# The last stage of a fused scan, attention and mixture-of-experts kernel: low parts moved to VectorE, gathered rows added tile by tile, last batch stored in four pieces

## The chip, the cores and the metric

One core of a Trainium2 chip. The metric is the device time of one execution in microseconds, as the median of three runs. The engines are TensorE (PE, with its weight loads as PEld), VectorE (DVE), ScalarE (ACT), GpSimd (POOL) and SyncE (SP), which issues most transfers.

## The reference, cut to what matters

Four batches of 512 rows, 512 wide. A selective scan over a context and an attention block come first; the change touches only what ends the program, the feed-forward part:

```
probs = softmax(h @ w_router); top_w, top_i = top_k(probs, 2)
y = (silu(h @ w_gate_e) * (h @ w_up_e)) @ w_down_e            # 8 experts, 352 wide
routed = sum over the 2 chosen experts of top_w * y
sh = (silu(h @ w_sh_gate) * (h @ w_sh_up)) @ w_sh_down        # shared expert, 1408 wide
x = x + routed + sigmoid(h @ w_sh_eg) * sh
out = x_before + tanh(g_ffn) * (that x)
```

## The kernel before, in words

**Numbers in two parts.** Each float32 operand of these products is split into a high part (rounded by ScalarE) and a low part (the value less the high part). A product is three passes: high by high, low by high, high by low. `split_product` (L627, matmuls at L631) issues them.

**The order of the feed-forward part.** The shared expert is 1408 wide, that is 11 pieces of 128. Nine of them come first (`NSB` = 3 passes), for all 16 row tiles (`NX` = 16, four per batch). Then follow 23 expert tiles of 256 routed rows (`NT` = 23), whose results go to the DRAM tensor `yg`. Then the last two pieces of the shared expert (`SHORT` = 2) are done batch by batch: eight steps s = 0 to 7, for batch b = s // 2. In each step `last_gate_up(s)` is two products of 12 matmuls on TensorE, `last_tanh(s)` runs on ScalarE, `last_act(s)` is two instructions on VectorE (L2174, L2179), `last_round(s)` writes the high part `lah` on ScalarE (L1655), and `last_rest(s)` writes the low part `lal` on GpSimd (L2464). `last_down(b)` is four tiles of six matmuls each. TensorE's order is: steps 0 to 3, down(0), steps 4 and 5, down(1), steps 6 and 7, down(2), down(3); one expert tile's down product lies behind step 0.

**The adding.** `shared_add(NSB, b)` (L2144) adds the four tiles of down(b) from two PSUM banks into the rows `xs`; a tile of `last_down` waits until the tile two before it has been added, since it writes the same bank (`pe.wait_ge(d_acc, m - 1)`, L1152). `combine(b)` (L2190) adds the two gathered expert rows of each row, eight instructions for a batch: all four tiles for the first choice, then all four for the second. It waits for all eight gathers of the batch (`y_in`).

**The gathers.** `gather(b, first, end_)` (L2471) issues indirect DMAs on GpSimd, two for each row tile, eight for a batch, 32 in all, into `yab`, which holds two batches. Batch 2 waits until batch 0 is combined, batch 3 until batch 1 is. GpSimd's order is: low parts 0 and 1, a wait for the last expert tile's store, gathers 1 to 4, low part 2, gathers 5 to 10, low part 3, gathers 11 to 16, low parts 4 and 5, gathers 17 to 24, low part 6, gathers 25 to 28, low part 7, gathers 29 to 32.

**VectorE's order.** Step 3 is followed by the adds of batch 0, step 4 by combine(0), step 5 by the adds and the combine of batch 1; steps 6 and 7 follow, then adds and combine of batch 2, then of batch 3.

**The stores.** SP stores each batch as one transfer of 1 MB (L619), when it is added and combined.

The names of the waits: `f_ah`, `f_al` count high and low parts, `f_a` the activations, `d_mm` and `d_acc` the down tiles made and added, `comb` the combine instructions.

Of the kernel before, what the change touches and what calls it, by code (L numbers as in the profile page):

```python
# [6 lines left out]
B, L, H = 4, 512, 512  # L7
# [7 lines left out]
T4 = L // P  # L15
KC = H // P
NCH = -(-EI // P)
SHORT = -(-SI // P) - (NU - NE - 1) * NCH
EW = NCH * P
NSH = NU - NE  # L20
NSB = NSH - 1
TT = 2 * P
NT = 2 * B * L // TT + NE - 1
NX = B * T4
# [19 lines left out]
def build(nc, x_in, ctx_in, gates_in, w_in_in, chan_in, xproj_in, dtproj_in, watt_in, bqk_in,  # L44
          bv_in, wln_in, route_in, wffn_in, rope_in, perm_in, ident_in, mask_in, iota_in, out,
          b_scratch, x2d, h2d, hhd, xg, yg):
    f32, f32r, bf16, u32, i32 = (mybir.dt.float32, mybir.dt.float32r, mybir.dt.bfloat16,
                                 mybir.dt.uint32, mybir.dt.int32)
    ALU, ACT, AX = mybir.AluOpType, mybir.ActivationFunctionType, mybir.AxisListType
# [3 lines left out]
    with ctx:  # L53
        def sem(name):
            return ctx.enter_context(nc.semaphore(name))
# [25 lines left out]
        sg = keep("sg", [P, NX])  # L81
# [12 lines left out]
        slot = keep("slot", [P, 2, NX], u32)  # L94
# [47 lines left out]
        rtw = mid("rtw", [P, KC, ROUTE])  # L142
        rth = mid("rth", [P, KC, ROUTE], f32r)
        rtl = mid("rtl", [P, KC, ROUTE], f32r)
# [92 lines left out]
        def xs_rows(first, last):  # L237

            if last <= EARLY * T4:
                return xs_early[:, first:last, :]  # L240
            return xs_late[:, first - EARLY * T4:last - EARLY * T4, :]

        def xs_row(t):
            return xs_rows(t, t + 1)[:, 0, :]
# [30 lines left out]
        hT_ready, y_acc, y_z, x1_done = sem("states_transposed"), sem("y_added"), sem("y_gated"), sem("x1_done")  # L275
        wraw_in = [sem("att_weights_loaded0"), sem("att_weights_loaded1")]
        wah_done, wal_done = sem("att_weights_hi"), sem("att_weights_lo")
        rt_split = sem("router_split")
        a_bn, a_mv, a_norm, a_hp = [sem("att_" + n) for n in ("stats", "meanvar", "norm", "scaled")]
        h1_mm, h1_hi, h1_lo = sem("h1_transposed"), sem("h1_hi"), sem("h1_lo")  # L280
        v_mm, v_done = sem("v_product"), sem("v_ready")
# [44 lines left out]
        def parts(u):  # L326
            return NCH if u < NSB else SHORT
# [24 lines left out]

        def last_step(u):
            return sum(parts(v) for v in range(u + 1)) * B

        def gate_up_split(e, job, c):
            if c < 2:
# [72 lines left out]
        def _(sp):  # L430
# [121 lines left out]
            def moe_stage():  # L552
# [57 lines left out]
                for b in range(1, B):  # L610
# [2 lines left out]
                        sp.dma_start(part[:].bitcast(f32), hhd[j, b]).then_inc(hh_ld[b], 16)  # L613
                    if b == 1:
                        tile_out(NT - 1)
                for b in range(B):
                    sp.wait_ge(comb, 2 * T4 * (b + 1))
                    sp.wait_ge(d_acc, NX * NSB + T4 * (b + 1))
                    sp.dma_start(out[b], xs_rows(T4 * b, T4 * b + T4)).then_inc(stored, 16)  # L619

            moe_stage()
            sp.wait_ge(stored, B * 16)

        @block.tensor
        def _(pe):
# [399 lines left out]
            shared = shared_pieces()  # L1026
            first_scan()
            pe.wait_ge(attc_in, 80)
            pe.wait_ge(rt_split, 2)
            pe.wait_ge(wal_done, KC)  # L1030
            for r in range(B):
                round_(r, r + 1)
# [156 lines left out]
        def _(act):  # L1189
# [507 lines left out]
            make_consts()  # L1697
            first_scan()
            act.wait_ge(attc_in, 80)
            nc.scalar.activation(rth[:], rtw[:], ACT.Copy).then_inc(rt_split, 1)  # L1700
            for r in range(B):
                round_(r, r + 1)
            for step in range(4):
# [5 lines left out]
        def _(dve):  # L1709
# [336 lines left out]
            def moe_stage():  # L2046
# [89 lines left out]
                def shared_add(u, b):  # L2136
                    for tt in range(T4):
                        m, t = NX * u + T4 * b + tt, T4 * b + tt
                        dve.wait_ge(d_mm, m + 1)
                        if m == T4 * EARLY:  # L2140
                            dve.wait_ge(xs_ld, 32 * B)
                        if u:
                            dve.wait_ge(d_acc, m - NX + 1)
                        nc.vector.scalar_tensor_tensor(xs_row(t), FD[m % 2][:], sg[:, t:t + 1], xs_row(t),  # L2144
                                                       ALU.mult, ALU.add).then_inc(d_acc, 1)
# [19 lines left out]
                def tile_out(i):  # L2165
                    dve.wait_ge(y_mm, 2 * i + 2)
                    if i >= 2:
                        dve.wait_ge(y_st[i % 2], 16 * (i // 2))
                    nc.vector.tensor_copy(ysb[:, i % 2, 1, :], FD[1][:]).then_inc(y_sv, 1)
# [8 lines left out]
                    dve.wait_ge(f_al, n - 1)  # L2178
                    nc.vector.tensor_tensor(fa[:, n % 2, :], FU[n % 2][:], ft[:, n % 2, :], ALU.mult).then_inc(f_a, 1)  # L2179

                def combine(b):
                    dve.wait_ge(y_in[b % 2], 16 * 2 * T4 * (b // 2 + 1))
                    for j in range(2):
                        for tt in range(T4):
                            t = T4 * b + tt
                            if j:
                                dve.wait_ge(comb, 2 * T4 * b + tt + 1)
                            else:
                                dve.wait_ge(d_acc, NX * NSB + t + 1)
                            nc.vector.scalar_tensor_tensor(xs_row(t), yab[:, b % 2, tt, j, :], w01[:, j, t:t + 1],  # L2190
                                                           xs_row(t), ALU.mult, ALU.add).then_inc(comb, 1)

# [18 lines left out]
                for i in range(NT):  # L2211
# [6 lines left out]
                    if i:  # L2218
                        tile_out(i - 1)
                    low_down(NSB + i + 1)  # L2220
                for s in range(SHORT * B):
                    last_act(s)
                    if s == 0:
                        tile_out(NT - 1)
                    if s == 3:
                        shared_add(NSB, 0)
                    if s == 4:
                        combine(0)
                    if s == 5:
                        shared_add(NSB, 1)  # L2230
                        combine(1)
                for b in range(2, B):
                    shared_add(NSB, b)
                    combine(b)

            dve.wait_ge(const_in, 96)
            dve.wait_ge(consts, 7)
# [2 lines left out]
                                        ALU.mult, ALU.mult).then_inc(consts, 1)  # L2240
            first_scan()
            dve.wait_ge(attc_in, 80)
            dve.wait_ge(rt_split, 1)
            nc.vector.tensor_tensor(rtl[:], rtw[:], rth[:].bitcast(f32), ALU.subtract).then_inc(rt_split, 1)
            dve.wait_ge(zfill, 16 * 12)
            dve.wait_ge(wal_done, KC)
            for r in range(B):
# [9 lines left out]
        def _(pool):  # L2257
# [179 lines left out]
            def moe_stage():  # L2437
# [22 lines left out]
                def last_rest(s):  # L2460
                    b, c = divmod(s, SHORT)
                    n = ENDING + s
                    pool.wait_ge(f_ah, n + 1)
                    nc.gpsimd.tensor_tensor(lal[:, b % 2, c, :], fa[:, n % 2, :], lah[:, b % 2, c, :].bitcast(f32),  # L2464
                                            ALU.subtract).then_inc(f_al, 1)

                def gather(b, first, end_):

                    for r in range(first, end_):
                        tt, j = divmod(r, 2)  # L2470
                        nc.gpsimd.indirect_dma_start(yab[:, b % 2, tt, j, :], None, yg, bass.IndirectOffsetOnAxis(  # L2471
                            ap=slot[:, j, T4 * b + tt:T4 * b + tt + 1], axis=0)).then_inc(y_in[b % 2], 16)

                for s, (u, b, c) in enumerate(steps):
                    if s < SE:
# [21 lines left out]
                last_rest(1)  # L2497
                for i in range(2):
                    pool.wait_ge(y_st[i], 16 * ((NT + 1 - i) // 2))
                gather(0, 0, 4)  # L2500
                last_rest(2)
                gather(0, 4, 8)
                gather(1, 0, 2)
                last_rest(3)
                gather(1, 2, 8)
                last_rest(4)
                last_rest(5)
                pool.wait_ge(comb, 2 * T4)
                gather(2, 0, 8)
                last_rest(6)  # L2510
                pool.wait_ge(comb, 4 * T4)
                gather(3, 0, 4)
                last_rest(7)
                gather(3, 4, 8)

            for row, value in ((mhalf, -0.5), (eps5, 1e-5), (eps6, 1e-6), (mone, -1.0), (perh, 1.0 / H),
                               (one, 1.0), (onee, 1.0 + 1e-6), (epsp, 1e-5 * 1e-6)):
# [86 lines left out]
```

## Time and profile before

| what | value |
|---|---|
| median of three runs | 1787.9 us (1785.01 to 1793.58) |
| the profiled execution | 1790.59 us |
| its span | 1788.8 us, so 1.8 us lie around it |
| mean granted TensorE clock | 0.902 |
| PE busy | 1503.7 us, 84% |
| DVE busy | 1166.9 us, 65% |
| ACT busy | 916.2 us, 51% |
| POOL busy | 810.2 us, 45% |

Busy shares are averages over stages that differ in what limits them. All that the change moves lies in the last 100 us of the span, so the rows below are of that stretch. In the timeline a row is: start, length, engine, line, operation, written tile, read tiles, shape and count; in brackets the idle time before it and what ended that.

### The profile page before, as it was taken

What the parts mean: (1) busy time and instruction counts of PE and PEld (TensorE: products, weight loads), DVE (VectorE), ACT (ScalarE), POOL (GpSimd) and SP (SyncE); (2) the same over time, 40 slices, a digit from 0 to 9 for tenths busy, and PEclk for the clock granted to TensorE, in tenths of its full rate; (3) what the DMA queues carried; (4) which work ended last, traced back from release to release, by engine and by line L of the source; (5) the groups of instructions that cost most, each with busy time, mean ns of one, the idle gap of its engine ahead of it and who ended that gap; (6) DMA issues with size and microseconds to landing.
All of it is one profiled execution on the core that took longest, in us unless ns stands there. A gap on an engine that the chain in (4) does not pass through costs nothing.

```text
span 1788.8 us, 26797 instructions
## 1 busy us (share of the span) xinstructions
PE 1503.7 (84%) x9168; PEld 1150.6 (64%) x9168; DVE 1166.9 (65%) x1699; ACT 916.2 (51%) x2038; POOL 810.2 (45%) x807
## 2 busy tenths in 40 slices
PE   5677967788777789677878998799999999999994
PEld 2344645565445556455655666688787999999973
DVE  5987589996699985899945444432324666566545
ACT  5675457764467753567724663221213666666510
POOL 1992266542466532565413211243422555555444
PEclk8789968899878899788988999899999999999997
DMA  4460001111011111011132004721311877777464
GB/s 168 153 229 19 25 23 55 54 43 54 7 35 55 54 36 31 19 47 54 37 123 95 30 32 160 293 77 59 110 37 65 307 243 253 261 241 253 155 221 165
DMA packets 94664, 195.76 MB, mean 109 GB/s; under 512 B 8945, under 2 KB 25841, under 8 KB 91201
## 3 DMA queue, kind: packets, MB, share of 16 engines
q1 hardware_dynamic: 89408, 177.26, 29.1%
q0 software_dynamic: 5120, 16.78, 2.8%
q8 instruction: 75, 1.23, 0.3%
q14 instruction: 61, 0.49, 0.1%
HBM read 140.40 MB, written 53.61 MB: 108 GB/s over the span
## 4 chain that ended last, share of the span: by engine, by line
PE 55%; DVE 16%; issue 15%; POOL 7%; ACT 5%; DMA 1%; SPq 1%; DVEq 0%; ACTq 0%; POOLq 0%
PE scores L631 21%; PE bank L631 14%; DVE HS L1770 6%; DVE YA L1781 4%; PE bank L705 3%; PE bank L775 3%; POOL GB L2281 2%; PE bank L790 2%; ACT bank L1269 2%; PE bank L825 2%; PE scores L762 2%; POOL yab L2471 2%; PE scores L749 1%; PE bank L1092 1%; PE scores L765 1%
## 5 line engine op out<-in xcount | busy, mean ns | idle before, releaser
L2281 POOL TENSOR_TENSOR GB<-DU,BB 128x512 f32<-128x512 f32 x256 | 326.8, 1298 | 36.1 <-DVE DL L1752 21.2
L1770 DVE TENSOR_TENSOR_SCAN HS<-bank,GB 128x512 f32<-128x512 f32 x224 | 272.0, 1214 | 20.3 <-ACT bank L1269 17.6
L705 PE MATMUL bank<-ident,HS 128*128 128x128 f32 x860 | 165.8, 325 | 120.9 <-DVE YA L1781 104.9
L705 PEld LDWEIGHTS bank<-ident,HS 128*128 128x128 f32 x860 | 115.2, 165 | 166.3 <-DVE YA L1781 129.8
L1269 ACT ACTIVATE bank<-DL,aneg 128x512 f32<-128x512 f32 x224 | 154.7, 691 | 110.0 <-DVE HS L1770 108.2
L775 PE MATMUL bank<-ident,EX 128*128 128x128 f32 x640 | 131.5, 306 | 34.2 <-ACT PT L1314 20.9
L631 PE MATMUL scores<-xth,wgh 128*128 128x256 f32 x552 | 158.1, 286 | 2.2 <-DVE fa L2162 1.3
L1781 DVE SCALAR_TENSOR_TENSOR YA<-bank,Ct,YA 128x512 f32<-128x512 f32 x199 | 147.0, 738 | 14.2 <-PE bank L705 12.8
L631 PE MATMUL scores<-xth,wgl 128*128 128x256 f32 x552 | 156.1, 283 | 0.0
L631 PE MATMUL scores<-xtl,wgh 128*128 128x256 f32 x552 | 156.1, 283 | 0.0
L1314 ACT ACTIVATE PT<-bank 128x128 f32<-128x128 f32 (+3 forms) x256 | 110.3, 431 | 72.0 <-PE bank L775 64.9
L1306 ACT ACTIVATE EX<-scores,nm 128x128 f32<-128x128 f32 (+3 forms) x256 | 132.3, 521 | 22.4 <-DVE nm L1826 21.7
L775 PEld LDWEIGHTS bank<-ident,EX 128*128 128x128 f32 x640 | 79.8, 154 | 75.0 <-issue 47.0
L2426 POOL TENSOR_TENSOR wgl<-wgr,wgh 128x768 fp32r<-128x768 f32 x54 | 110.9, 2057 | 30.4 <-ACT wgh L1580 30.4
L2443 POOL TENSOR_TENSOR fal<-fa,fah 128x512 fp32r<-128x512 f32 x30 | 38.8, 1293 | 162.7 <-ACT fah L1609 162.5
L2324 POOL TENSOR_TENSOR ctl<-cn,cth 128x128 fp32r<-128x128 f32 x64 | 29.3, 458 | 180.7 <-ACT cth L1325 180.7
L631 PEld LDWEIGHTS scores<-xth,wgh 128*128 128x128 f32 x552 | 105.7, 191 | 3.6 <-DVE fa L2162 1.7
L631 PE MATMUL scores<-hah,wgh 128*128 128x512 f32 x272 | 106.7, 392 | 1.0 <-issue 1.0
L631 PE MATMUL scores<-hal,wgh 128*128 128x512 f32 x272 | 106.5, 391 | 0.0
L631 PE MATMUL scores<-hah,wgl 128*128 128x512 f32 x272 | 106.3, 391 | 0.0
L631 PEld LDWEIGHTS scores<-xtl,wgh 128*128 128x128 f32 x552 | 105.7, 192 | 0.9
L631 PEld LDWEIGHTS scores<-xth,wgl 128*128 128x128 f32 x552 | 105.7, 191 | 0.0
(294 smaller groups left out, 3798.6 us busy)
## 6 DMA issues: line engine op xcount, KB each, us to landing
wgr<-wffn_in SPq DMA_DIRECT2D x108, 384.0 KB, 6.5
wdr<-wffn_in SPq DMA_DIRECT2D x81, 256.0 KB, 3.1
BB<-b_scratch SPq DMA_DIRECT2D x64, 256.0 KB, 3.3
xr<-xg SPq DMA_DIRECT2D x23, 512.0 KB, 5.8
yg<-ysb SPq DMA_DIRECT2D x23, 512.0 KB, 6.5
xg<-V SPq DMA_DIRECT2D x11, 1024.0 KB, 5.8
hah<-hhd SPq DMA_DIRECT2D x5, 1024.0 KB, 14.1
hal<-hhd SPq DMA_DIRECT2D x5, 1024.0 KB, 16.1
```

What stands on the lines that cost most here:

```text
L631: mm = nc.tensor.matmul(out_, parts[a](k), rhs_parts[b](k), start=(k == 0 and j == 0), stop=(k == n - 1 and j == 2))
L705: mm = nc.tensor.transpose(state_bank(s, q)[:, et * P:(et + 1) * P], HS[:, n % 2, et, tt * P:(tt + 1) * P], ident[:])
L762: nc.tensor.matmul(SB[:, a, 0:W], QK[r:r + HD, m, i * P:(i + 1) * P], QK[r:r + HD, 4 + m, 0:W], start=True, stop=False)
L775: mm = nc.tensor.transpose(turned_bank(b, v)[:, kb * P:(kb + 1) * P], EX[:, a, kb * P:(kb + 1) * P], ident[:])
L1269: nc.scalar.activation(decay_bank(s, k), DL[:, et, :], ACT.Exp, scale=aneg[:, et, n:n + 1]).then_inc(dA_ready, 1)
L1306: nc.scalar.activation(EX[:, a, 0:W], SB[:, a, 0:W], ACT.Exp, bias=nm[:, a:a + 1], accum_out=rs[:, q % 2, a:a + 1]).then_inc(ex_done, 1)
L1314: nc.scalar.activation(PT[:, a, 0:W], turned_bank(b, v)[:, 0:W], ACT.Copy).then_inc(pt_done, 1)
L1770: nc.vector.tensor_tensor_scan(HS[:, n % 2, et, :], decay_bank(s, k), GB[:, k % 4, :], 0.0, ALU.mult, ALU.add).then_inc(scan_done, 1)
L1781: nc.vector.scalar_tensor_tensor(YA[:, tt, :], state_bank(s, q), Ct[:, tt, n:n + 1], YA[:, tt, :], ALU.mult, ALU.add).then_inc(y_acc, 1)
L2281: nc.gpsimd.tensor_tensor(GB[:, k % 4, :], DU[:, et, :], BB[:, n % 2, :], ALU.mult).then_inc(gb_ready, 1)
L2426: nc.gpsimd.tensor_tensor(wgl[raw][:, c, :], wgr[raw][:, c * 2 * EW:(c + 1) * 2 * EW], wgh[raw][:, c, :].bitcast(f32), ALU.subtract).then_ ...
L2443: nc.gpsimd.tensor_tensor(fal[:, b % 2, c, :], fa[:, s % 2, :], fah[:, b % 2, c, :].bitcast(f32), ALU.subtract).then_inc(f_al, 1)
```

## The change

It does five things, all in the last stage.

1. Low parts 2 to 7 (`last_rest`) run on VectorE; parts 0 and 1 stay on GpSimd, ahead of the gathers.
2. GpSimd issues its 32 gathers without other work between them. A gather for batch 2 or 3 waits only for the same tile of the batch two before.
3. `combine` works tile by tile (both choices of one row tile after another), and its tiles are put between steps, low parts and adds in an order written out by hand. For batch 2 the combine comes before the add of the down product, for the others behind it.
4. The very last gather has a semaphore of its own, `y_last`, waited for only ahead of the very last combine instruction. To have one free, the two increments of `rt_split`, early in the program, go to `consts`.
5. Batch 3 is stored as four transfers of one row tile (256 KB), each as soon as its tile is done.

```diff
+        def added_first(t):
+            return t < 2 * T4 or t >= NX - T4
...
-                for b in range(B):
+                for b in range(B - 1):
                     sp.wait_ge(comb, 2 * T4 * (b + 1))
                     sp.wait_ge(d_acc, NX * NSB + T4 * (b + 1))
                     sp.dma_start(out[b], xs_rows(T4 * b, T4 * b + T4)).then_inc(stored, 16)
+                for t in range(NX - T4, NX):
+                    sp.wait_ge(comb, 2 * t + 2)
+                    sp.wait_ge(d_acc, NX * NSB + t + 1)
+                    sp.dma_start(out[B - 1, :, t % T4:t % T4 + 1, :], xs_rows(t, t + 1)).then_inc(stored, 16)
...
-            pe.wait_ge(rt_split, 2)
+            pe.wait_ge(consts, 7 + T4 + 2)
...
-                def combine(b):
-                    dve.wait_ge(y_in[b % 2], 16 * 2 * T4 * (b // 2 + 1))
-                    for j in range(2):
-                        for tt in range(T4):
-                            t = T4 * b + tt
+                def last_rest(s):
+                    b, c = divmod(s, SHORT)
+                    n = ENDING + s
+                    dve.wait_ge(f_ah, n + 1)
+                    dve.wait_ge(f_al, n)
+                    nc.vector.tensor_tensor(lal[:, b % 2, c, :], fa[:, n % 2, :], lah[:, b % 2, c, :].bitcast(f32),
+                                            ALU.subtract).then_inc(f_al, 1)
+
+                def add_last(b, first, end_):
+                    for t in range(T4 * b + first, T4 * b + end_):
+                        m = NX * NSB + t
+                        dve.wait_ge(d_mm, m + 1)
+                        if added_first(t):
+                            dve.wait_ge(d_acc, m - NX + 1)
+                        else:
+                            dve.wait_ge(comb, 2 * t + 2)
+                        nc.vector.scalar_tensor_tensor(xs_row(t), FD[m % 2][:], sg[:, t:t + 1], xs_row(t),
+                                                       ALU.mult, ALU.add).then_inc(d_acc, 1)
+
+                def combine(b, first, end_):
+                    dve.wait_ge(y_in[b % 2], 16 * (2 * T4 * (b // 2 + 1) - (b == B - 1)))
+                    for tt in range(first, end_):
+                        t = T4 * b + tt
+                        dve.wait_ge(d_acc, NX * (NSB if added_first(t) else NSB - 1) + t + 1)
+                        for j in range(2):
                             if j:
-                                dve.wait_ge(comb, 2 * T4 * b + tt + 1)
-                            else:
-                                dve.wait_ge(d_acc, NX * NSB + t + 1)
+                                dve.wait_ge(comb, 2 * t + 1)
+                            if j and t == NX - 1:
+                                dve.wait_ge(y_last, 16)
...
-                for s in range(SHORT * B):
+                last_act(0)
+                tile_out(NT - 1)
+                for s in range(1, 4):
                     last_act(s)
-                    if s == 0:
-                        tile_out(NT - 1)
-                    if s == 3:
-                        shared_add(NSB, 0)
-                    if s == 4:
-                        combine(0)
-                    if s == 5:
-                        shared_add(NSB, 1)
-                        combine(1)
-                for b in range(2, B):
-                    shared_add(NSB, b)
-                    combine(b)
+                last_rest(2)
+                add_last(0, 0, 4)
+                last_rest(3)
+                combine(0, 0, 2)
+                last_act(4)
+                combine(0, 2, 3)
+                last_rest(4)
+                combine(0, 3, 4)
+                last_act(5)
+                add_last(1, 0, 1)
+                last_rest(5)
+                add_last(1, 1, 4)
+                combine(1, 0, 3)
+                last_act(6)
+                combine(1, 3, 4)
+                last_rest(6)
+                combine(2, 0, 2)
+                last_act(7)
+                add_last(2, 0, 1)
+                last_rest(7)
+                combine(2, 2, 3)
+                add_last(2, 1, 3)
+                combine(2, 3, 4)
+                add_last(2, 3, 4)
+                add_last(3, 0, 4)
+                combine(3, 0, 4)
...
                 last_rest(1)
                 for i in range(2):
                     pool.wait_ge(y_st[i], 16 * ((NT + 1 - i) // 2))
-                gather(0, 0, 4)
-                last_rest(2)
-                gather(0, 4, 8)
...
-                last_rest(7)
-                gather(3, 4, 8)
+                for b in range(B):
+                    for tt in range(T4):
+                        if b >= 2:
+                            pool.wait_ge(comb, 2 * (T4 * (b - 2) + tt) + 2)
+                        gather(b, 2 * tt, 2 * tt + 2)
```

## Rows read from the trace of the kernel before

**Rows 1.** The chain that ended last, 1756 to 1789 us, shares by line.
```profile
by line: issue 35.0%; POOL yab L2471 25.3%; DVE xs_late L2190 14.3%; DMA yab<-yg,slot 10.4%; POOL lal L2464 7.7%; DVEq L53 2.0%; POOLq L53 0.7%
```

**Rows 2.** Timeline of GpSimd: low parts and gathers.
```profile
1705.63 1.29 POOL L2464 TENSOR_TENSOR lal<-fa,lah 128x512 fp32r<-128x512 f32 x1 [8.23 <-ACT lah L1655]
1707.07 0.99 POOL L2471 DMA_INDIRECT yab<-yg,slot  x1 [0.15 <-issue]
...
1710.90 0.96 POOL L2471 DMA_INDIRECT yab<-yg,slot  x1 [0.30 <-issue]
...
1715.86 0.94 POOL L2471 DMA_INDIRECT yab<-yg,slot  x1 [0.30 <-issue]
1723.63 0.94 POOL L2471 DMA_INDIRECT yab<-yg,slot  x1 [6.83 <-issue]
...
1731.42 1.02 POOL L2471 DMA_INDIRECT yab<-yg,slot  x1 [0.30 <-issue]
...
1740.30 0.95 POOL L2471 DMA_INDIRECT yab<-yg,slot  x1 [5.28 <-issue]
...
1757.89 0.95 POOL L2471 DMA_INDIRECT yab<-yg,slot  x1 [4.85 <-issue]
...
1775.66 0.95 POOL L2471 DMA_INDIRECT yab<-yg,slot  x1 [5.01 <-issue]
```

**Rows 3.** Timeline of VectorE: adds, combines and the last steps.
```profile
1715.69 1.51 DVE L2144 SCALAR_TENSOR_TENSOR xs_early<-bank,sg,xs_early 128x512 f32<-128x512 f32 x2
...
1727.52 6.08 DVE L2190 SCALAR_TENSOR_TENSOR xs_early<-yab,w,xs_early 128x512 f32<-128x512 f32 x8 [0.50 <-DMA yab<-yg,slot]
...
1749.04 0.69 DVE L2174 SCALAR_TENSOR_TENSOR ft<-ft,scores 128x512 f32<-128x512 f32 x1
1749.76 0.69 DVE L2179 TENSOR_TENSOR fa<-scores,ft 128x512 f32<-128x512 f32 x1
...
1761.22 6.74 DVE L2190 SCALAR_TENSOR_TENSOR xs_late<-yab,w,xs_late 128x512 f32<-128x512 f32 x8 [3.47 <-DMA yab<-yg,slot]
...
1779.11 5.39 DVE L2190 SCALAR_TENSOR_TENSOR xs_late<-yab,w,xs_late 128x512 f32<-128x512 f32 x8 [3.98 <-DMA yab<-yg,slot]
```

**Rows 4.** Timeline of TensorE: matmuls around its waits in the last stage.
```profile
1735.64 0.50 PE L631 MATMUL bank<-wdh,lah 128*128 128x512 f32 x1 [2.54 <-DVE xs_early L2144]
...
1740.09 0.40 PE L631 MATMUL scores<-hah_odd,wgh 128*128 128x512 f32 x1
...
1750.98 0.39 PE L631 MATMUL bank<-wdh,lah 128*128 128x512 f32 x1
...
1766.99 0.77 PE L631 MATMUL bank<-wdh,lah 128*128 128x512 f32 x1 [10.02 <-POOL lal L2464]
...
1771.47 0.39 PE L631 MATMUL bank<-wdh,lah 128*128 128x512 f32 x1
...
1773.96 0.39 PE L631 MATMUL bank<-wdh,lal 128*128 128x512 f32 x1
```

**Rows 5.** Stretches: busy time of each engine, granted clock, DMA share, GB/s.
```profile
1740.00:1751.00 11.00, 11.00 (x51) 9.07 (x50) 7.43 (x11) 1.12 (x2) 9.01 (x9) 1.00 0.39 108
...
1767.00:1771.00 4.00, 4.00 (x10) 3.16 (x11) 1.71 (x3) 0.00 (x0) 3.03 (x3) 0.56 0.60 174
```

**Rows 6.** Groups by line in the last stage: the low part on GpSimd, and VectorE's nearest.
```profile
L2464 POOL TENSOR_TENSOR lal<-fa,lah 128x512 fp32r<-128x512 f32 x8 | 10.3, 1290 | 13.4 <-ACT lah L1655 13.4
...
L2043 DVE TENSOR_TENSOR wdl<-wdr,wdh 128x512 fp32r<-128x512 f32 x2 | 1.3, 689 | 0.0
```

**Rows 7.** Timeline of SP's transfers in the last stage.
```profile
1713.72 0.32 SPq L613 DMA_DIRECT2D hah_odd<-hhd  x1
...
1733.63 15.86 SPq L619 DMA_DIRECT2D out<-xs_early  x2
1767.99 16.88 SPq L619 DMA_DIRECT2D out<-xs_late  x2
```

**Rows 8.** Transfers of line 487, 256 KB each, whole span.
```profile
DMA to landing us min/median/max: 2.2/3.5/4.4
```

More of the change, by code:

```diff
@@ L277, in build @@
         wah_done, wal_done = sem("att_weights_hi"), sem("att_weights_lo")
-        rt_split = sem("router_split")
+        y_last = sem("last_row_gathered")
         a_bn, a_mv, a_norm, a_hp = [sem("att_" + n) for n in ("stats", "meanvar", "norm", "scaled")]
@@ L619, in moe_stage @@
                     sp.dma_start(out[b], xs_rows(T4 * b, T4 * b + T4)).then_inc(stored, 16)
+                for t in range(NX - T4, NX):
+                    sp.wait_ge(comb, 2 * t + 2)
+                    sp.wait_ge(d_acc, NX * NSB + t + 1)
+                    sp.dma_start(out[B - 1, :, t % T4:t % T4 + 1, :], xs_rows(t, t + 1)).then_inc(stored, 16)
             moe_stage()
-            sp.wait_ge(stored, B * 16)
+            sp.wait_ge(stored, (B - 1 + T4) * 16)
         @block.tensor
@@ L1699, in _ @@
             act.wait_ge(attc_in, 80)
-            nc.scalar.activation(rth[:], rtw[:], ACT.Copy).then_inc(rt_split, 1)
+            nc.scalar.activation(rth[:], rtw[:], ACT.Copy).then_inc(consts, 1)
             for r in range(B):
@@ L2242, in _ @@
             dve.wait_ge(attc_in, 80)
-            dve.wait_ge(rt_split, 1)
-            nc.vector.tensor_tensor(rtl[:], rtw[:], rth[:].bitcast(f32), ALU.subtract).then_inc(rt_split, 1)
+            dve.wait_ge(consts, 7 + T4 + 1)
+            nc.vector.tensor_tensor(rtl[:], rtw[:], rth[:].bitcast(f32), ALU.subtract).then_inc(consts, 1)
             dve.wait_ge(zfill, 16 * 12)
@@ L2471, in gather @@
                         nc.gpsimd.indirect_dma_start(yab[:, b % 2, tt, j, :], None, yg, bass.IndirectOffsetOnAxis(
-                            ap=slot[:, j, T4 * b + tt:T4 * b + tt + 1], axis=0)).then_inc(y_in[b % 2], 16)
+                            ap=slot[:, j, T4 * b + tt:T4 * b + tt + 1], axis=0)).then_inc(y_last if (b, r) == (B - 1, 2 * T4 - 1) else y_in[b % 2], 16)
                 for s, (u, b, c) in enumerate(steps):
@@ L2499, in moe_stage @@
                     pool.wait_ge(y_st[i], 16 * ((NT + 1 - i) // 2))
-                gather(0, 0, 4)
-                last_rest(2)
-                gather(0, 4, 8)
[L2503 to L2512, printed above, removed]
-                last_rest(7)
-                gather(3, 4, 8)
+                for b in range(B):
[3 more added lines that the diff above has]
+                        gather(b, 2 * tt, 2 * tt + 2)
             for row, value in ((mhalf, -0.5), (eps5, 1e-5), (eps6, 1e-6), (mone, -1.0), (perh, 1.0 / H),
```

## The prediction

> **What bounds the kernel now.** I read first the chain that ended last, because the change lies wholly in the last 100 us. Over the final 33 us [rows 1] TensorE is not in it at all: issuing on GpSimd and the gathers hold most, VectorE's combine 14.3%, GpSimd's low parts 7.7%. So the question is GpSimd's queue, and its timeline was next [rows 2]. Gathers follow one another at about 1.28 us (1707.07 to 1710.90 is three steps), except that gathers 8, 16, 24 and 32 each stand behind 4.85 to 6.83 us of idle time which no semaphore of the program explains. Those four rows are the clock of the ending. They lie 16.7, 17.6 and 17.8 us apart. In the first of these cycles GpSimd does one low part between gathers, in the other two it does two each, at 1.29 us [rows 6].
>
> What follows from the late gathers is read in VectorE's and TensorE's timelines. Combine(2) starts at 1761.22, 3.33 us behind gather 24, combine(3) at 1779.11, 3.45 us behind gather 32 [rows 2, 3]. TensorE stands 10.02 us ahead of down(3), for low part 7 [rows 4], which waits on GpSimd behind gather 28. TensorE ends at 1774.35 (1773.96 + 0.39), so the last 14.4 us are gather 32, eight combines (5.39 us) and a 1 MB store: 1784.50 to 1788.8, 4.3 us [rows 2 to 4]. SP issues the four stores in those places [rows 7].
>
> TensorE itself needs less. 48 matmuls from 1740.09 to 1750.98 are 0.227 us each; a down tile of six is 1.36, a step of 24 is 5.44.
>
> **The change part by part.**
>
> *The semaphore of the router split*: same producers, same order, one count shared. It adds no instruction; zero. What covers it is nothing, and nothing is needed.
>
> *Low parts 2 to 7 on VectorE*: nearest row is VectorE's own subtraction of this shape, 0.69 us [rows 6]. Six of them are 4.1 us more on VectorE, and 6 x 1.29 = 7.7 us off GpSimd. Where VectorE is idle they cost nothing. Part 2 is the first that shows: it stands between step 3 and the first add of batch 0, so the add at 1715.69 [rows 3] comes 0.7 later and TensorE's third tile of down(0) with it, 0.7 us. TensorE has slack for that, since what ends the program comes from the gathers.
>
> *The gathers*: gather 1 stays at 1707.07, for low part 1 ahead of it stays on GpSimd [rows 2]. Gather 7 moves from 1715.86 to 1707.07 + 6 x 1.27 = 1714.7. The stall ahead of gather 8 spans the loads of `hah_odd` (2 MB, issued from 1713.72 [rows 7]); with the stall unchanged gather 8 is at 1714.7 + 0.94 + 6.83 = 1722.5, with the shortest stall (4.85) at 1720.5, with no gain at 1723.6. I take 1722.5, as the loads stay where they were.
>
> A cycle of eight gathers is then 7 x 1.27 + 0.95 = 9.85 us plus the stall. The stall is not shown without a store beside it. From below: data land about 3.4 us after a gather's start, 2.5 after its end, so 2.5 is the least if the stall waits for the seventh to land: cycle 12.4. From above: 5.28 gives 15.1. The 1 MB stores still fall near gathers 16 and 24, so I stay nearer the upper rows: 14.2. Gather 16 then starts at 1736.7, gather 24 at 1750.9, gather 32 at 1765.1, against 1740.3, 1757.9 and 1775.7.
>
> *What VectorE does with it.* In tile order the second instruction of a pair waits for the first to end. The pair of a step shows that price: 0.72 from start to start (1749.04, 1749.76) for an instruction of 0.69; a combine lasts 0.75, so about 0.78 and then 0.66 (5.39 less 0.75, over seven), 1.44 a tile, 5.8 a batch instead of 5.4 [rows 3]. Combine(0) can start at 1722.5 + 3.9 = 1726.4 and holds step 4 until 1729.3; TensorE is then in step 5 until 1731. Its third tile of down(1) waits for the add that stands behind step 5, to about 1736.5, much as at 1735.64 before [rows 4]. Combine(1) starts at about 1740, step 6 at 1746.5, step 7's product ends at 1751.5. So nothing up to there is later than the gathers by more than a microsecond, and TensorE's idle time of 2.5 us returns.
>
> The new wait is combine(2, 0, 2): it stands ahead of step 7 in VectorE's queue. Behind it are step 7, the first add of batch 2 and low part 7, and on them wait the third tile of down(2), ScalarE's high part, and down(3). All start from gather 24: 1750.9 + 3.4 = 1754.3. From there, in order:
> - two tiles of combine 2.9, step 7 1.4, add 0.75, restart 0.05: TensorE starts the third tile at 1759.4, after some 5 us of idle time;
> - 12 matmuls after such a gap took 1766.99 to 1771.47, 4.5 us instead of 2.7, the granted clock 0.56 in that stretch [rows 4, 5], between the levels of 1.2 and 2.4 GHz; between the two tiles lies the wait for an add behind low part 7 and a combine, 0.6; then four tiles, 5.45: 1769.9;
> - visible end and last add, 0.2 + 0.7: 1770.8;
> - four tiles of combine(3), 5.8: 1776.6. `y_last` comes at 1765.1 + 3.45 = 1768.6 and is not waited for;
> - the last store is 256 KB. Such a transfer took at least 2.2 us [rows 8], against 4.3 for 1 MB: 1778.8.
>
> The median of line 487 is 3.5 [rows 8], but beside other traffic; at the end only the three small stores ahead of it run, so I take 2.2 and keep 3.5 for the range.
>
> Sum: span 1778.8 against 1788.8, 10.0 us less (0.56%). Split: 2.1 from the store, 7.9 from where the combine of batch 3 starts (1770.8 against 1779.1, less 0.4 for tile order). The profiled execution was 1790.59 with 1.8 around the span; the median of the runs is 1787.9. So 1777.9, written as 1778.
>
> A rule that speaks against the change concerns the last term but one. The row first: gathers beside combines last 1.02 us (1731.42) against 0.94 alone, and two batches of combines took 6.08 and 6.74 us against 5.39, each with a GpSimd low part beside them [rows 2, 3]. So here GpSimd's subtraction delays VectorE by 0.7 to 1.4, and a gather loses 0.08 at most. The Trainium skill (SBUF — State Buffer, Who interferes with whom) says that a VectorE instruction with two SBUF inputs contends with a GpSimd instruction that reads SBUF, and that the second one blocks fully. By it the combines gain (the subtractions are gone from GpSimd), and gathers, if they read their row numbers through that way, would each lose a whole VectorE instruction; and the sum by it would be 1790.6 with one instruction each.
>
> **The rivals.**
> - *Gathers 16 and 24 gain only the low parts, and stores hit them as hard as the stores of before* (cycle 15.1 to 16.7, or the clock staying low into down(3)). For: every stall seen has a store or load beside it. Against: the store of batch 0 now leaves near 1734, when gather 15 has mostly landed. With 16.7 twice, gather 24 is at 1755.9 and the end at 1783.8; time 1783, no measurable change. Chance 0.32, with the milder form of the next rival but one in it.
> - *The stall is mostly the stores*, and away from them it is 2.5 to 3.5 us: cycle 12.4 to 13.3, gather 24 at 1747.3 to 1749.1, TensorE's gap shrinks to 2 or 3 us, end 1774.9 to 1777; time 1775. Chance 0.14.
> - *Slower: gathers blocked by VectorE.* VectorE now runs six more instructions with two SBUF inputs, and often two behind one another without a gap (1.44 us for a tile of combine). If each of the 16 gathers between 8 and 24 is held for such a pair, that is 16 x 1.44 = 23 us: combine(2) starts at 1777.3 and the end is 1801.8, time 1801. With one instruction of 0.74 each it is 11.8 us, end 1790.6, time 1790, no change to measure. It eats the gain from 10.0 / 16 = 0.63 us per gather and decides for slower from (10.0 + 8.9) / 16 = 1.2. For it stand the stretched combines, against it the 0.08 seen on gathers. Chance of the slower form 0.07.
> - *The change frees nothing*, since the stalls are not work of GpSimd: then only the 7.7 us of subtractions go, which is what the forecast counts; the store alone is worth 2.1 (1786). Contained in the first rival.
>
> **How the numbers follow.** The forecast has 0.47: 1778, own range 1775 to 1782. A measurement of this kernel can tell about 0.5%, 8.9 us, so faster means below 1779.0. The second rival is faster; of the forecast's own spread some four fifths lies below that line. Faster 0.53, same 0.40, slower 0.07. For the range 1773 takes in the shorter cycle, 1786 the first rival with the store of 3.5 us; outside are the slower rival and some tails.
>
> **What the profile after would show.** GpSimd: 32 gathers, still with a stall at 8, 16, 24 and 32, the cycles 13.3 to 15.1, gather 24 before 1753. VectorE: combine(2)'s first instruction waiting for the gathers and starting near 1754. TensorE: one gap of 4 to 6 us ahead of the third tile of down(2), none ahead of down(3), end near 1770. Four stores of 256 KB, the last landing 2.2 us behind the last combine. It is wrong if the stalls grow when gathers are issued closer together, if gathers last over 1.1 us, if the last combine waits for `y_last`, or if TensorE's clock stays at the lower level for the six last tiles.

## The result and the profile after

The changed kernel took 1782.4 us (median of eight), the kernel before 1790.97 beside it; the ratio is 0.996, with an interval of 0.9944 to 0.9976. So it is faster by 0.4%, clear of noise but under the 0.5% that the prediction took as the bound: by that bound the time is the same, which had a chance of 0.40, and not faster, which had 0.53. Forecast were 10.0 us less. The profiled execution has a span of 1783.5 us, 5.3 less than before.

Executions differ by several microseconds ahead of the last stage: in the traces of this study step 0 starts anywhere between 1683.7 and 1694.1 us, in kernels that differ up to there in no more than one semaphore, the places of small tiles and the descriptor space. So I compare **the ending**: from the first matmul of step 0 to the end of the span. (That matmul starts 0.19 us ahead of VectorE's copy of the expert tile before, which is easy to find in each trace.) Before it is 1687.7 to 1788.8, 101.1 us; after it is 1688.8 to 1783.5, 94.7 us. The change is worth 6.4 us of the forecast 10.0.

GpSimd's timeline after, which answers to [rows 2]:

```profile
1708.17 0.99 POOL L2517 DMA_INDIRECT yab<-yg,slot  x1 [0.15 <-issue]
...
1715.75 0.95 POOL L2517 DMA_INDIRECT yab<-yg,slot  x1 [0.30 <-issue]
1724.57 0.94 POOL L2517 DMA_INDIRECT yab<-yg,slot  x1 [7.88 <-issue]
...
1728.32 1.32 POOL L2517 DMA_INDIRECT yab<-yg,slot  x1 [0.30 <-issue]
...
1738.66 0.94 POOL L2517 DMA_INDIRECT yab<-yg,slot  x1 [3.42 <-issue]
...
1752.09 1.43 POOL L2517 DMA_INDIRECT yab<-yg,slot  x1 [3.18 <-issue]
...
1765.60 0.95 POOL L2517 DMA_INDIRECT yab<-yg,slot  x1 [3.25 <-issue]
```

The stalls are still ahead of gathers 8, 16, 24 and 32, but three of them are 3.2 to 3.4 us instead of 5. The cycles are 14.1, 13.4 and 13.5 us. In the ending's own time gather 24 stands at 63.3 (forecast 63.2, before 70.2).

The chain of waits after, from gather 24 to the combine of batch 3 (start, length, what):

```profile
1748.92 3.18 issue
1752.09 5.96 DMA yab<-yg,slot
...
1758.08 0.76 DVE xs_late L2220
...
1758.86 1.42 DVE xs_late L2220 x2
...
1760.38 0.60 issue
1760.98 0.69 DVE ft L2182
...
1761.84 0.47 issue
1762.31 0.75 DVE xs_late L2206
...
1763.10 11.19 PE bank L639 x36
...
1774.35 0.63 issue
1774.99 0.75 DVE xs_late L2220
```

This is the path of the prediction, link by link: gather 24, two tiles of combine, step 7, one add, then 36 matmuls (six tiles) and the last batch. One link is far longer than forecast: the gather took 5.96 us to land, not 3.4. SP's timeline says what was beside it:

```profile
1735.90 16.56 SPq L623 DMA_DIRECT2D out<-xs_early  x2
1769.68 0.33 SPq L623 DMA_DIRECT2D out<-xs_late  x1
1776.54 4.68 SPq L627 DMA_DIRECT2D out<-xs_late  x4
```

The first row is two stores. The second of them ends its issue at 1735.90 + 16.56 = 1752.46, and an issue lasts 0.33: batch 1's 1 MB leaves at 1752.13, within 0.1 us of gather 24's start. TensorE after, answering to [rows 4], and two stretches answering to [rows 5]:

```profile
1737.91 0.80 PE L639 MATMUL bank<-wdh,lah 128*128 128x512 f32 x1 [3.09 <-DVE xs_early L2206]
...
1763.10 0.79 PE L639 MATMUL bank<-wdh,lah 128*128 128x512 f32 x1 [7.01 <-DVE xs_late L2206]
...
1773.89 0.39 PE L639 MATMUL bank<-wdh,lal 128*128 128x512 f32 x1
```

```profile
1757.00:1767.00 10.00, 3.90 (x9) 2.69 (x10) 8.57 (x13) 0.63 (x1) 5.08 (x6) 0.57 0.56 180
1767.00:1771.00 4.00, 4.00 (x16) 3.21 (x15) 2.73 (x4) 0.00 (x0) 0.00 (x0) 0.80 0.40 135
```

The wait ahead of down(3) has gone and one of 7.01 us stands ahead of down(2)'s third tile, on VectorE's add. The granted clock is 0.57 in the stretch that holds it, and 0.50, the lower level, from 1763.1 to 1768.0. The last combine and the landing of the small stores:

```profile
1774.99 5.88 DVE L2220 SCALAR_TENSOR_TENSOR xs_late<-yab,w,xs_late 128x512 f32<-128x512 f32 x8
```

```profile
DMA to landing us min/median/max: 2.2/2.2/2.3
```

VectorE ends at 1780.87, the span 2.6 us later.

### The profile page after: what moved, and what is told of

Its sections match the earlier page's. It is cut to its first block, busy times and chain, and to the rows that moved or that the text cites. A ratio compares the mean times of both kernels' runs of the same rounds, so it can differ in the third digit from the quotient of the medians.

```text
span 1783.5 us, 26815 instructions
## 1 busy us (share of the span) xinstructions
PE 1498.1 (84%) x9168; PEld 1147.3 (64%) x9168; DVE 1171.1 (66%) x1705; ACT 915.1 (51%) x2038; POOL 803.1 (45%) x801
## 3 DMA queue, kind: packets, MB, share of 16 engines
q8 instruction: 75, 1.23, 0.3%
## 4 chain that ended last, share of the span: by engine, by line
PE 55%; DVE 17%; issue 14%; ACT 6%; POOL 5%; DMA 2%; SPq 1%; DVEq 0%; ACTq 0%; POOLq 0%
PE scores L639 21%; PE bank L639 15%; DVE HS L1778 6%; DVE YA L1789 4%; PE bank L713 3%; PE bank L783 3%; PE bank L798 2%; PE scores L770 2%; ACT bank L1277 2%; PE bank L833 2%; POOL GB L2327 2%; POOL yab L2517 1%; PE scores L757 1%; PE bank L1100 1%; DVE nm L1834 1%
## 6 DMA issues: line engine op xcount, KB each, us to landing
hah<-hhd SPq DMA_DIRECT2D x5, 1024.0 KB, 14.2
```

## The experiments

The table gives the ratio to the kernel before, its interval, and the ending of the profiled execution. The experiments follow in the order of what they tell.

| kernel | ratio | interval | ending, us | gather 24 | TensorE ends |
|---|---|---|---|---|---|
| before | 1 | | 101.1 | 70.2 | 86.7 |
| after | 0.996 | 0.9944 to 0.9976 | 94.7 | 63.3 | 85.5 |
| late_store | 0.9943 | 0.993 to 0.9956 | 92.0 | 63.5 | 82.7 |
| step7_first | 0.9924 | 0.9908 to 0.994 | 88.0 | 63.3 | 78.5 |
| step7_late_store | 0.9941 | 0.9912 to 0.997 | 88.1 | 63.4 | 78.6 |
| low_parts_only | 0.9972 | 0.9956 to 0.9988 | 96.2 | 62.3 | 85.9 |
| tile_stores_only | 1.0003 | 0.9989 to 1.0018 | 100.2 | 70.1 | 86.6 |
| ring_before_b | 0.9923 | 0.9902 to 0.9944 | 91.1 | 58.5 | 80.7 |
| ring_after | 0.9889 | 0.9871 to 0.9907 | 83.5 | 49.5 | 74.2 |
| ring_order | 0.99 | 0.9882 to 0.9918 | 84.5 | 52.4 | 75.0 |
| ring_comb3 | 0.9888 | 0.9862 to 0.9913 | 81.3 | 49.7 | 75.7 |

(The last two columns are in the ending's own time.)

Each ending is that of one execution. `before` and `tile_stores_only` are alike up to the last store, and their gather 32 stands at 88.0 and 88.5, so differences of half a microsecond between endings mean nothing. The ratios are of all runs; the two measures differ by up to 3.8 us (ring_before_b: 13.8 us by its ratio, 10.0 in the ending), which is as wide as the intervals. Three more versions, ring16, ring16b and ring_before, had only four of the eight small tiles elsewhere; they did not fit in SBUF and have no time.

**late_store: is it the store that holds gather 24 back?**

```diff
                 for b in range(B - 1):
+                    if b == 1:
+                        sp.wait_ge(y_in[0], 16 * 4 * T4)
```

> The kernel after, but SP issues batch 1's store only when gather 24 has landed. Measured by the length of the ending, from the first matmul of step 0 to the end of the span: 101.1 us before (1687.7 to 1788.8), 94.7 after (1788.8 to 1783.5 with a start at 1688.8). Theory 'the store hits gather 24': in the profile after, gather 24 and the 1 MB store of batch 1 start together at 1752.1 and the combine waits 5.96 us for the gather instead of the 3.4 of an undisturbed one; without the store beside it combine(2) starts 2.6 us earlier and the ending is 92.1. Rival 'VectorE holds the gather back' (gather 24 lasted 1.43 us beside a low part and combine): the landing stays near 6 us and the ending at 94.7.

The ending is 92.0, against 92.1 forecast. The gather and the combine behind it:

```profile
1751.07 0.94 POOL L2519 DMA_INDIRECT yab<-yg,slot  x1 [3.34 <-issue]
```

```profile
1751.07 3.29 DMA yab<-yg,slot
```

The start of gather 24 has not moved (63.5 against 63.3); its landing takes 3.29 us instead of 5.96. The gather itself also lasts 0.94 here and not 1.43, for its neighbours on VectorE have moved too; the landing of 5.96 counts from the gather's start, so the 0.5 of the longer issue can be part of it. The pair step7_first and step7_late_store below has no such difference: there gather 24 lasts 0.95 and 0.94, and it lands after 4.8 us with batch 1's store issued 0.65 us ahead of it, after 3.3 without:

```profile
DMA to landing us min/median/max: 4.8/4.8/4.8
```

```profile
DMA to landing us min/median/max: 3.3/3.3/3.3
```

So the store is the cause, of 1.5 us in that pair and of 2.2 to 2.7 here.

**step7_first: is it VectorE's order that makes the gather matter?**

```diff
         def added_first(t):
-            return t < 2 * T4 or t >= NX - T4
+            return True
...
-                combine(2, 0, 2)
                 last_act(7)
                 add_last(2, 0, 1)
                 last_rest(7)
-                combine(2, 2, 3)
-                add_last(2, 1, 3)
-                combine(2, 3, 4)
-                add_last(2, 3, 4)
-                add_last(3, 0, 4)
+                add_last(2, 1, 4)
+                combine(2, 0, 2)
+                add_last(3, 0, 1)
+                combine(2, 2, 3)
+                add_last(3, 1, 2)
+                combine(2, 3, 4)
+                add_last(3, 2, 4)
                 combine(3, 0, 4)
```

> The kernel after, but on VectorE step 7, its low part and the adds of batch 2 stand ahead of combine(2), and all adds come before the combines. Theory 'VectorE's order makes TensorE wait for gather 24': TensorE's 7.0 us of idle time ahead of the third tile of down(2) shrinks to under 1 us and its lower clock goes, down(3) ends near 1765 instead of 1774.3; combine(2) (5.8), four adds (2.8) and combine(3) (5.8) follow from the gather's landing at 1758, then a store of 2.6: ending 86.3, 8.4 less. Rival 'the gathers alone set the end': ending 94.7 as after.

88.0, 6.7 less than after, of the 8.4 expected. TensorE's long wait has gone:

```profile
1768.85 0.50 PE L639 MATMUL bank<-wdh,lah 128*128 128x512 f32 x1 [1.68 <-DVE xs_late L2206]
```

That is the only wait over 1 us left behind down(1), now in down(3), for an add that stands behind two tiles of combine. TensorE ends at 78.5 instead of 85.5. This wait is not what the forecast missed. Combine(2) starts at 71.0 in the ending's time, where the forecast had gather 24's landing (1758 in after, 69.2), because it stands behind the fourth add of batch 2, which waits for TensorE:

```profile
1764.49 0.75 DVE L2206 SCALAR_TENSOR_TENSOR xs_late<-bank,sg,xs_late 128x512 f32<-128x512 f32 x1 [0.62 <-PE bank L639]
1765.16 2.98 DVE L2220 SCALAR_TENSOR_TENSOR xs_late<-yab,w,xs_late 128x512 f32<-128x512 f32 x4
```

From there to its end VectorE shows no idle time, so these 1.8 us account for the 1.7 that are missing.

**step7_late_store: are these two causes or one?** Both edits together.

> Both edits on the kernel after: step 7, its low part and batch 2's adds ahead of combine(2), and batch 1's store only when gather 24 has landed. With the order alone the ending was 88.0, with combine(2) starting at 71.0 and TensorE waiting 1.7 us ahead of down(3)'s third tile. Theory 'two causes, partly the same wait': combine(2) starts at 66.8, that wait goes, TensorE ends at 76.8, ending 86.3. Rival 'independent': 88.0 less the 2.8 of the store, 85.2. Rival 'the store no longer matters': 88.0.

88.1 against 88.0: with step 7 ahead, the store's collision costs nothing. The rival that the store no longer matters holds, and my own forecast of 86.3 was wrong: combine(2) started at 71.0 and 71.1, since it now waits for the fourth add of batch 2 and not for the gather. The 1.8 us that I expected did not come; TensorE's wait in down(3) is still there (1.67), beside a VectorE that is busy throughout.

**low_parts_only: what do the low parts bring without the new order?**

```diff
                 for s in range(SHORT * B):
                     last_act(s)
+                    if s >= 2:
+                        last_rest(s)
...
-                gather(0, 0, 4)
-                last_rest(2)
...
+                for b in range(B):
+                    if b >= 2:
+                        pool.wait_ge(comb, 2 * T4 * (b - 1))
+                    gather(b, 0, 8)
```

> The kernel before with one part of the change: low parts 2 to 7 on VectorE, each right behind its step, and GpSimd with only gathers between, a batch at a time; VectorE's order, the combine and the stores are those of before. Theory 'the gain is the gathers', the new order takes part of it back': gather 24 at about 51 to 53 us of the ending's start plus 12, as after; steps 6 and 7 stand ahead of combine(2) as before, so TensorE does not wait for it; combine(3) starts when gather 32 lands: ending 90, 11 less than before's 101.1 and 4.7 less than after's. Rival 'the order by tiles brings the gain': ending over 96.

96.2: the theory's 90 fell by 6.2, and the number is the rival's (over 96), though not for the rival's reason, as the parts add up below. Gather 24 is as early as after (62.3), but does not set the end:

```profile
1736.40 0.50 PE L631 MATMUL bank<-wdh,lah 128*128 128x512 f32 x1 [4.04 <-DVE xs_early L2144]
...
1765.93 0.79 PE L631 MATMUL bank<-wdh,lah 128*128 128x512 f32 x1 [4.09 <-DVE xs_late L2144]
```

TensorE waits twice for an add behind a whole combine, 4.0 and 4.1 us, with a granted clock of 0.66 and 0.50 in the 3.6 and 4.0 us behind them. I had left both out of the 90. So this part alone gives 4.9 of the 6.4 us.

**tile_stores_only: what does the store in four pieces bring?** The kernel before, with batch 3 stored in four pieces.

```diff
+                for t in range(NX - T4, NX):
+                    sp.wait_ge(comb, 2 * NX - T4 + t % T4 + 1)
+                    sp.wait_ge(d_acc, NX * NSB + t + 1)
+                    sp.dma_start(out[B - 1, :, t % T4:t % T4 + 1, :], xs_rows(t, t + 1)).then_inc(stored, 16)
```

> The kernel before with one part of the change: batch 3 stored by four transfers of 256 KB, the combine unchanged (all first choices, then all second, so the four tiles end 0.66 us apart). From the last combine's end to the end of the span it was 4.3 us before and 2.64 after. Theory: 2.6 to 2.8, ending 99.4 to 99.6 instead of 101.1. Rival (four transfers issued within 2 us stand behind each other): no gain, 101.

From the last combine's end to the end of the span it is 2.85 us, against 4.3 before: 1.45 less. In this execution gather 32 came 0.6 later, so the ending shows 0.9. The ratio, 1.0003, can't tell so little from nothing. Adding the parts: 96.2 less 1.5 is 94.7, the ending after. So by this subtraction the new order of VectorE, with the descriptor space as it was, added nothing; no run has the order alone.

**ring_after: what are the stalls?** Nothing of the program's order is changed; eight small tiles are placed elsewhere to free 1 KB a partition.

```diff
-    nc = bacc.Bacc("TRN2", target_bir_lowering=False, num_devices=1, dynamic_dma_scratch_size=1024)
+    nc = bacc.Bacc("TRN2", target_bir_lowering=False, num_devices=1, dynamic_dma_scratch_size=2048)
```

```profile
1711.62 0.95 POOL L2517 DMA_INDIRECT yab<-yg,slot  x1 [0.30 <-issue]
1712.87 1.30 POOL L2517 DMA_INDIRECT yab<-yg,slot  x1 [0.30 <-issue]
1714.48 0.94 POOL L2517 DMA_INDIRECT yab<-yg,slot  x1 [0.30 <-issue]
...
1736.71 1.23 POOL L2517 DMA_INDIRECT yab<-yg,slot  x1 [1.56 <-DVE xs_early L2220]
```

No stall is left ahead of 8, 16, 24 or 32; each follows at 0.30 us. Gather 24 starts at 49.5 instead of 63.3, and the ending is 83.5, lower than the 87 to 89 expected. TensorE's waits behind step 5 are 0.48, 0.90 and 1.18 us, and the granted clock is 1.00 until TensorE ends. So the stalls were lack of descriptor space, and the order that the change wrote is good once gathers come early. No run has the tiles elsewhere with 1024 bytes.

What ends a stall can be read from the landings, in the five traces with 1024 bytes that have them (times in us from the span's start):

| run, gather ahead of the stall | starts | lands after | landed | next gather starts |
|---|---|---|---|---|
| late_store, 7 (2 MB of loads beside it) | 1714.55 | 8.40 | 1722.95 | 1723.53 |
| late_store, 15 | 1732.95 | 3.91 | 1736.87 | 1737.44 |
| late_store, 23 | 1746.78 | 3.71 | 1750.50 | 1751.07 |
| tile_stores_only, 15 (1 MB store beside it) | 1732.18 | 5.68 | 1737.85 | 1738.43 |
| tile_stores_only, 31 (1 MB store beside it) | 1767.71 | 6.04 | 1773.75 | 1774.33 |

The first and the fourth row, as the trace has their landings:

```profile
DMA to landing us min/median/max: 8.4/8.4/8.4
```

```profile
DMA to landing us min/median/max: 5.7/5.7/5.7
```

In all 20 stalls of these traces the next gather starts 0.57 to 0.59 us behind the landing of the gather just ahead of the stall. So the space is free again only when the last of the gathers that filled it has landed, and whatever delays that one gather, a store or the loads, lengthens the stall. That speaks against the places of the tiles as the cause. With 2048 bytes one trace shows the same thing small: in ring_order gather 15 stands behind 0.81 us of idle time and starts 0.59 behind the landing of gather 8.

**ring_before_b: how much was the space to the kernel before?** The same edit on the kernel before.

> The kernel before with 2048 bytes a partition for GpSimd's descriptors and nothing of the change. The kernel after with that space had an ending of 83.5 us and stalls of 0.3 us. Theory 'descriptor space was the larger part of what the change worked around': no stalls; low part 7 done within 3 us of step 7, TensorE's 10 us wait ahead of down(3) goes, combine(3) follows down(3): ending 86 to 90 instead of 101.1, so more than the whole change brings (94.7), and the change then adds 3 to 6 us. Rival 'the low parts among the gathers are the cause': low part 7 still late, TensorE waits over 5 us, ending over 96.

91.1, a little above the expected 86 to 90: 10.0 us less than before, against 6.4 of the whole change. The rival falls; low part 7 is no longer late:

```profile
1752.42 1.30 POOL L2464 TENSOR_TENSOR lal<-fa,lah 128x512 fp32r<-128x512 f32 x1
...
1761.46 0.71 PE L631 MATMUL bank<-wdh,lah 128*128 128x512 f32 x1 [4.08 <-DVE xs_late L2144]
```

What is left is the wait of 4.08 us for an add behind combine(2), as in low_parts_only. On top of the space the change is worth 91.1 - 83.5 = 7.6 us, more than the 3 to 6 expected.

**ring_order: is there a better order with that space?** The space, all adds first, and this order from step 4 on:

```diff
+                last_act(4)
+                last_rest(4)
+                combine(0, 0, 3)
+                last_act(5)
+                add_last(1, 0, 1)
+                last_rest(5)
+                add_last(1, 1, 2)
+                combine(0, 3, 4)
+                add_last(1, 2, 4)
+                combine(1, 0, 3)
+                last_act(6)
+                last_rest(6)
+                combine(1, 3, 4)
+                last_act(7)
+                add_last(2, 0, 1)
+                last_rest(7)
+                add_last(2, 1, 3)
+                combine(2, 0, 2)
...
```

> The kernel after with 2048 bytes a partition for GpSimd's descriptors, all adds ahead of the combines of their batch, and VectorE's order rewritten so that steps 4 to 7 and each add that TensorE waits for stand ahead of combines that wait for gathers. Theory: TensorE's 3 us wait in down(1) and the 7 us wait in down(2) go, it ends near 70 us of the ending, VectorE's own work behind step 7 (16 us) is the bound: ending 81, 13.7 less than after and 20 less than before. Rival (gathers still set the pace because stores and loads take the transfer rate): ending 86 or more.

84.5, 3.5 above the expected 81 and under the rival's 86: better than after by 10.2, worse than ring_after by 1.0 (the ratios, 0.99 and 0.9889, can't tell the two apart). My order leaves VectorE idle where ScalarE rounds (0.70 us ahead of a low part, twice) and lets TensorE wait 1.70 and 1.66 us. ring_after shows that it was not needed.

**ring_comb3: is VectorE's own work the bound then?** The space, and for batch 3 each tile combined ahead of its add.

```diff
-            return t < 2 * T4 or t >= NX - T4
+            return t < 2 * T4
...
-                add_last(3, 0, 4)
-                combine(3, 0, 4)
+                for tt in range(T4):
+                    combine(3, tt, tt + 1)
+                    add_last(3, tt, tt + 1)
```

> The kernel after with 2048 bytes a partition for GpSimd's descriptors, and for batch 3 each tile combined ahead of its add (as the change does for batch 2). With the space alone the ending was 83.5, of which the eight combines behind the last add are 5.9 and VectorE stands idle four times for 0.6 to 0.85 us before it. Theory 'behind the stalls VectorE's own work is the bound': from the last add of batch 2 four tiles of 1.44 + 0.7, then the store: ending 80.5 to 81.5. Rival: the adds, now behind combines, hold TensorE's last tiles and the ending stays at 83 or more.

81.3, in the expected range, 19.8 less than before. TensorE now waits 0.64 us twice in down(3) and ends 1.5 later than in ring_after, but the combines are done by then. The ratio is 0.9888 (0.9862 to 0.9913), not to be told from ring_after's.

## Why the prediction was right, point by point

The time lay in the range and the direction was right; the size was 6.4 where 10.0 was forecast, and 1782.4 lies just outside the forecast's own 1775 to 1782. The path was the one forecast, link by link. By its own terms:

- *Gather 8*: forecast 34.8 in the ending's time, measured 35.8. The stall ahead of it grew to 7.88 instead of staying at 6.83: gather 7 started 1.2 us earlier in the ending's time, but it lands only when the loads of 2 MB beside it let it (8.4 us in late_store), so issuing it earlier brought 0.1 us.
- *The cycle of eight gathers*: 14.2 forecast, 14.1, 13.4 and 13.5 measured. The reading from below (12.4) and above (15.1) held, and so did its condition, that the stall waits for the seventh gather to land. The stall itself was taken as 4.35 and is 3.2 to 3.4; the gathers and the gaps between them were taken as 9.85 and are 10.3 to 10.7. Gather 24 was right to 0.1 us by luck: the forecast was 1.0 too early at gather 8 and 0.9 too long over the two cycles.
- *The landing of gather 24*: **this term was mis-sized**, "gather 24 at 1750.9 + 3.4". It took 5.96, 2.6 more. The prediction had counted stores beside the stalls, from the rows in which they stood there before, and then used the undisturbed landing for the one transfer that a store did meet. late_store shows it: 2.7 us of the ending back from that edit alone.
- *From there to TensorE's restart*: 5.1 forecast, 5.0 measured.
- *TensorE's six tiles*: 10.7 with the visible end, measured 11.2; its wait was 7.0 and not 5, and the granted clock behind it was 0.50 until 1768.0.
- *Add and combine*: 6.5 forecast, 6.6 measured (1774.30 to 1780.87).
- *The last store*: 2.2 forecast from the landing, 2.6 measured to the end of the span. The landing is 2.2, as line 487 had it [rows 8], and 0.4 lies ahead of the issue and behind the landing. The 4.3 of before was taken with these in, so the saving of 2.1 was compared unlike; it is 1.7.
- The misses add up: 0.1 (gather 24) + 2.6 + 0.5 + 0.1 + 0.4 less 0.1 is 3.6, the difference of 10.0 and 6.4.

*The rivals.* That "stores hit them as hard as the stores of before" had 0.32 and named 1783: right in the time and in the culprit, but not in the place. The stalls shrank and the cycles stayed under its 15.1; the hit was the landing. "The stall is mostly the stores" had 0.14 and was right about the stall: away from the stores it is 3.2 to 3.4, in its 2.5 to 3.5, and the stalls of before were longer because gathers 15, 23 and 31 landed beside a store (after 5.7, 5.1 and 6.0 us in tile_stores_only, which has the gathers of before; after 3.6 to 4.0 in late_store, step7_first and step7_late_store, but for one of 5.6 with no store beside it, gather 31 of step7_late_store, which stays unexplained). Its end of 1775 did not come, for the cycles were 13.4 to 14.1 and not 12.4 to 13.3, and gather 24 met a store. The slower rival fell: gathers beside a VectorE instruction with two SBUF inputs lasted 1.11 us on average (13 of them, longest 1.43), the other 19 lasted 0.95. That is 0.16 each, far below the 0.63 at which the gain would have gone. The prediction's "a gather loses 0.08 at most" was misread from one row; the trace of before has four gathers of 1.23 to 1.37, all beside a combine and three of them right behind a low part, such as gather 17:

```profile
1743.95 1.37 POOL L2471 DMA_INDIRECT yab<-yg,slot  x1 [0.16 <-issue]
```

"The change frees nothing" was wrong in its split: of the shorter cycles, 1.3 to 2.5 are low parts and 1.7 to 1.9 the stall (5.28, 4.85 and 5.01 to 3.42, 3.18 and 3.25), with 0.2 to 0.5 lost again in longer gathers.

*What the forecast had seen only half.* It named combine(2, 0, 2) ahead of step 7 as the new wait and priced it, but did not ask what the order costs against another. step7_first answers: 6.7 us of the ending. And the four stalls were taken as given; they are 17.7 us of GpSimd's time after, and their removal is worth 11.2 to the changed kernel and 10.0 to the one before.

*What stays open.* Why a full space waits for the last of its transfers and not for the oldest is not shown, and sizes other than 1024 and 2048 bytes were not tried. By which of the shared resources a 1 MB store holds a gather back was only seen in the times, not separated.
